# Two-layer graph kernel: beta added in the first layer, closing normalisation in two fused passes, last four tiles normalised where they are made, transposes issued ahead of the closing stores

## The reference, cut to what matters

```
h = relu(layernorm(x))
x = x + quantised_gnn(h, adj)                      # layer 0, gives x1
h = relu(layernorm(x))
for s in range(2):                                 # layer 1
    A  = softmax of the top-p entries of (Xa W1 W2)(Xa W3)^T
    Xf = R @ Xf ; Xa = A @ Xa
    Z  = Z + Xf @ U1s[s] + Xa @ U2s[s]
Y = h + Z
out = x1 + (Y - mean(Y)) * rsqrt(var(Y) + 1e-5) * gamma + beta
```

## Time and profile before

| | |
|---|---|
| median of 3 runs | 1310.68 us |
| lowest, highest | 1308.89, 1313.84 us |
| the profiled execution's own time | 1313.01 us |
| its span, first to last instruction | 1311.2 us |
| PE busy | 1116.9 us (85%) |
| DVE busy | 1036.7 us (79%) |
| ACT busy | 442.7 us (34%) |
| POOL busy | 260.5 us (20%) |
| chain that ended last | DVE 49%, PE 31%, issue 10%, ACT 4%, DMA 4% |

### The profile page before, as it was taken

One profiled execution on the slowest core, in us unless ns is written; L12 is line 12 of the kernel. 1 busy time (PEld: TensorE's weight loads), 2 busy tenths in 40 slices (PEclk: granted clock), 3 DMA queues, 4 the chain that ended last, 5 costly groups with the idle time before them and its releaser, 6 DMA issues.

```text
span 1311.2 us, 16604 instructions
## 1 busy us (share of the span) xinstructions
PE 1116.9 (85%) x5402; PEld 515.1 (39%) x5402; DVE 1036.7 (79%) x2199; ACT 442.7 (34%) x836; POOL 260.5 (20%) x234
## 2 busy tenths in 40 slices
PE   0567999999999798899997998989995997898374
PEld 0223555554334344344443443334442443343131
DVE  7887777762798998888884019979989998998777
ACT  2544545455533134444331255631420521100000
POOL 6023323231312112012121113122110121111011
PEclk9888999999999899899998999999997999899786
DMA  6126656552424531533524433176633733733576
GB/s 235 63 83 214 234 184 223 171 188 72 140 85 147 127 74 41 105 73 65 138 57 96 82 113 118 60 256 178 136 104 86 166 89 99 174 95 100 172 210 203
DMA packets 190931, 172.19 MB, mean 131 GB/s; under 512 B 144704, under 2 KB 144704, under 8 KB 186752
## 3 DMA queue, kind: packets, MB, share of 16 engines
q1 hardware_dynamic: 190848, 171.23, 45.6%
HBM read 88.10 MB, written 49.55 MB: 105 GB/s over the span
## 4 chain that ended last, share of the span: by engine, by line
DVE 49%; PE 31%; issue 10%; ACT 4%; DMA 4%; SPq 1%; POOL 1%; DVEq 1%; POOLq 0%; ACTq 0%
DVE cand L1679 7%; DVE WS L1461 6%; PE UB L745 5%; DVE WS L1676 5%; DVE E L1692 5%; DVE WS L1684 4%; PE AB L735 3%; PE AB L728 3%; DVE g L1541 3%; PE RB L745 3%; PE RB L912 3%; DVE E L1691 3%; PE XB L745 2%; PE AB L912 2%; DVE cand L1719 2%
## 5 line engine op out<-in xcount | busy, mean ns | idle before, releaser
L1541 DVE TENSOR_REDUCE g<-E 128x1 f32<-128x2048 f32 x32 | 73.0, 2281 | 96.9 <-ACT E L1135 96.7
L1461 DVE SCALAR_TENSOR_TENSOR WS<-E,g 128x2048 bf16<-128x2048 f32 x48 | 120.5, 2553 | 0.4
L632 POOL TENSOR_TENSOR RT<-RT,AD 128x512 f32<-128x512 f32 x32 | 57.4, 1792 | 293.2 <-ACT RT L1194 293.1
L1679 DVE MAX8 cand<-WS 128x8 f32<-128x128 f32 x512 | 102.1, 277 | 1.1
L1135 ACT ACTIVATE E<-LB 128x512 f32<-128x512 f32 x128 | 75.4, 593 | 75.7 <-PE LB L835 60.4
L912 PE MATMUL AB<-VR,turns 128*128 128x512 f16 x256 | 67.0, 409 | 33.2 <-DMA turns<-E 33.2
L912 PE MATMUL RB<-VR,turns 128*128 128x512 f16 x256 | 64.1, 395 | 30.7 <-DMA turns<-E 30.7
L1684 DVE SCALAR_TENSOR_TENSOR WS<-E,g 128x2048 f32<-128x2048 f32 x33 | 81.1, 2456 | 0.9
L1171 ACT ACTIVATE E<-E,nmx 128x2048 f32<-128x2048 f32 x32 | 63.7, 1993 | 46.7 <-DVE nmx L1542 46.6
L912 PE MATMUL RB<-XR,turns 128*128 128x512 f16 x256 | 63.8, 394 | 17.8 <-DMA turns<-E 17.8
L1692 DVE SCALAR_TENSOR_TENSOR E<-WS,E 128x2048 f16<-128x2048 f32 x32 | 77.9, 2433 | 1.1
(11 more groups left out here) (307 smaller groups left out, 2174.5 us busy)
## 6 DMA issues: line engine op xcount, KB each, us to landing
turns<-adj_parts SPq DMA_DIRECT2D x48, 512.0 KB, 3.8
E<-adjT SPq DMA_DIRECT2D x16, 1024.0 KB, 7.6
adj_parts<-turns SPq DMA_DIRECT2D x16, 1024.0 KB, 5.2
AH<-adj_parts SPq DMA_DIRECT2D x16, 512.0 KB, 4.1
z_d<-UO SPq DMA_DIRECT2D x31, 256.0 KB, 2.3
XR<-x SPq DMA_DIRECT2D x4, 1024.0 KB, 11.8
WS<-U SPq DMA_DIRECT2D x4, 1024.0 KB, 7.7
x_d<-E SPq DMA_DIRECT2D x16, 256.0 KB, 2.0
```

What stands on the lines that cost most here:

```text
L1461: return v.scalar_tensor_tensor(junk[t % 2], e, g4[:, k, t:t + 1], e, op, ALU.mult, accum_out=g4[:, F_, t:t + 1])
L1541: ct(v.tensor_reduce(row(A2)[:, t:t + 1], E[:, slot, :], AX.X, ALU.max))
L1679: i = v.max(cand[:, t, 8 * c:8 * c + 8], WS[:, c * PART:(c + 1) * PART])
```

## The change

**Beta.** beta is loaded at the start of the program (into `XHL`). In layer 0 a new POOL step `x1_beta` adds it to x1 of each tile (into `X1B`, which is `WF`), and SP stores that sum in place of x1. It stands in POOL's loop between the root and `x_lo`. DVE's next tile waits for this step instead of the store. The DVE additions of beta at the end are gone.

**Closing passes.** A tile's last four element-wise steps become two: `(y - mean) * gamma`, which doesn't need the root, and `y * root + (x1 + beta)`. Both are `scalar_tensor_tensor`, one instruction per tile.

**Last four tiles.** Tiles 12 to 15 aren't stored and loaded again. ACT and POOL write them to `UO` and `XF` in turn, and DVE normalises each there as a batch of one (`end`). Their x1 is loaded once into `WS` (`end_in`). DVE's order is batch 0, batch 1, tile 12, batch 2, tiles 13, 14, 15. ACT waits, for tiles 14 and 15, until the store of tile 12 or 13 has read the buffer.

**SP's order in the last group.** The first loads no longer wait for all tiles to be kept (`s_kept, 2 * T`), only for the transposes of the group before; `order` has memory of its own now, and gamma goes to `WF`. The store of batch 0 comes after the transposes of tile 13, and the loads of batch 2 and the store of batch 1 after those of tile 14.

**The register load.** DVE no longer waits for the group's first mask ahead of the register load; that wait now stands behind the skipped piece.

```
-        gb = sb("gb", [P, 2, D], F32)
-        gam, bet = gb[:, 0, :], gb[:, 1, :]
-        order = gb[:, :, :].rearrange("p a d -> p (a d)").bitcast(F16)
+        order = sb("order", [P, N], F16)[:, :]
+        bet, X1B = XHL[:, :, :].rearrange("p h d -> p (h d)").bitcast(F32), WF
+        gam, ends = WF, (UO, XF)
...
             u_in(0)
+            sp.dma_start(bet, beta.partition_broadcast(P)).then_inc(s_gb, 16)
...
             def l0_stores(t):
-                sp.wait_ge(s_x1, t + 1)
-                sp.dma_start(x1_d[t], X1T).then_inc(s_x1out, 16)
+                sp.wait_ge(s_x1b, t + 1)
+                sp.dma_start(x1_d[t], X1B[:, :]).then_inc(s_x1out, 16)
...
+            def end_in():
+                sp.wait_ge(s_kept, 2 * T)
+                sp.dma_start(end_x, x1_d[T - G:T].rearrange("t p d -> p t d")).then_inc(s_endx, 16)
+
+            def end_out(t, nth):
+                sp.wait_ge(s_res, nth)
+                sp.dma_start(out[t], ends[t % 2][:, :]).then_inc(s_end[t % 2], 16)
...
                 if last:
-                    sp.wait_ge(s_kept, 2 * T)
-                    sp.dma_start(bet, beta.partition_broadcast(P)).then_inc(s_gb, 16)
-                    sp.dma_start(gam, gamma.partition_broadcast(P)).then_inc(s_gb, 16)
+                    sp.wait_ge(s_wl, T)
+                    sp.wait_ge(s_gb, 16)
+                    sp.dma_start(gam[:, :], gamma.partition_broadcast(P)).then_inc(s_gb, 16)
...
-                    if s and t < T - 1:
+                    if s and not last:
                         y_store(t)
+                    if last and i == 0:
+                        end_in()
+                        fin_out(0, 1)
                     if last and i == 1:
-                        fin_out(0)
                         fin_in(2)
-                        fin_out(1)
+                        fin_out(1, 2)
                     if last and i == 2:
-                        fin_in(3)
-                        fin_in(4)
+                        end_out(T - G, 3)
+                        fin_out(2, 4)
+                    if last and i == 3:
+                        end_out(T - G + 1, 5)
...
+            def x1_beta(t):
+                pool.wait_ge(s_x1, t + 1)
+                pool.wait_ge(s_x1out, 16 * t + OPEN)
+                q.tensor_tensor(X1B[:, :], X1T, bet, ALU.add).then_inc(s_x1b, 1)
+
             def l0_tile(t):
                 l0(t)
+                x1_beta(t)
                 x_lo(t, of(XR, t))
...
-                    act.wait_ge(s_yout, 16 * t + OPEN)
-                    a(UO[:, :], bank[:, :], ACT.Copy, scale=rden[:, slot:slot + 1]).then_inc(s_ue, 1)
+                    act.wait_ge(s_yout, 16 * min(t, T - G) + OPEN)
+                    if t >= T - G + 2:
+                        act.wait_ge(s_end[t % 2], 16)
+                    y = ends[t % 2] if t >= T - G else UO
+                    a(y[:, :], bank[:, :], ACT.Copy, scale=rden[:, slot:slot + 1]).then_inc(s_ue, 1)
...
-                dve.wait_ge(s_x1out, 16 * t + OPEN)
+                dve.wait_ge(s_x1b, t)
...
-                ct(masked(tiles[0][0], 0, THR))
+                ct.free(masked(tiles[0][0], 0, THR))
+                first_kept = ct.base + ct.n
...
+                dve.wait_ge(c_dve, first_kept)
                 for slot, t in tiles:
...
+                for k, (m, y, x1) in enumerate(tiles):
+                    (ch if k == n - 1 else ch.free)(v.scalar_tensor_tensor(y, y, mv[:, m, 0:1], gam[:, :], ALU.subtract,
+                                                                           ALU.mult))
+                dve.wait_ge(s_frs, nth)
+                for k, (m, y, x1) in enumerate(tiles):
+                    i = v.scalar_tensor_tensor(y, y, frs[:, m:m + 1], x1, ALU.mult, ALU.add)
+                i.then_inc(s_res, 1)
...
+            batch(0, 1)
+            batch(1, 2)
+            dve.wait_ge(s_endx, 16)
+            end(T - G, 3)
+            batch(2, 4)
+            for k in range(1, G):
+                end(T - G + k, 4 + k)
```

More of the change, by code:

```diff
@@ L179, in build @@
         ZT = Khl[:, 0, 0:2 * D].bitcast(F32)
-        FIN = [(G * b, G * b + G) for b in range(NG - 1)] + [(T - G, T - 1), (T - 1, T)]
+        BATCHES = NG - 1
         fin_y = [E[:, 2 * h, :].rearrange("p (t d) -> p t d", t=G) for h in range(2)]
@@ L244, in build @@
             "s_zin", "s_y", "s_yout", "s_fvar", "s_frs", "s_res", "s_out")]
-        s_finx, s_finy = ([sem(f"{n}{h}") for h in range(2)] for n in ("s_finx", "s_finy"))
+        s_finx, s_finy, s_end = ([sem(f"{n}{h}") for h in range(2)] for n in ("s_finx", "s_finy", "s_end"))
+        s_endx = sem("s_endx")
         s_xin = [sem(f"s_xin{b}") for b in range(NG)]
@@ L665, in pairs @@
                         continue
+                    if g == NG - 1 and i == 0:
+                        root(0, 0, G)
+                    y = ends[t % 2] if g == NG - 1 else UO
                     pool.wait_ge(s_zin, 16 * t + 16)
                     pool.wait_ge(s_ue, t + 2 * T + 1 + OPEN)
-                    q.tensor_tensor(UO[:, :], UO[:, :], ZT, ALU.add).then_inc(s_y, 1)
+                    q.tensor_tensor(y[:, :], y[:, :], ZT, ALU.add).then_inc(s_y, 1)
                     if g == NG - 1:
-                        for b in ((i,) if i < G - 1 else (i, i + 1)):
-                            pool.wait_ge(s_fvar, b + 1)
-                            m = slice(*FIN[b])
-                            q.tensor_tensor(frs[:, m], frs[:, m], powc[:, 0, m], ALU.pow).then_inc(s_frs, 1)
+                        if i == 0:
+                            root(1, G, 2 * G)
+                        root(2 + i + (i > 0), t, t + 1)
+                        if i == 0:
+                            root(3, 2 * G, 3 * G)
             def last_post():
@@ new lines, in batch, with end @@
+            def batch(b, nth):
+                dve.wait_ge(s_finx[b % 2], 16 * (b // 2) + 16)
+                dve.wait_ge(s_finy[b % 2], 16 * (b // 2) + 16)
+                normed([(G * b + t, fin_y[b % 2][:, t, :], fin_x[b % 2][:, t, :]) for t in range(G)], nth)
+            def end(t, nth):
+                dve.wait_ge(s_y, t + 1 + OPEN)
+                normed([(t, ends[t % 2][:, :], end_x[:, t - (T - G), :])], nth)
+            dve.wait_ge(s_gb, 32)
+            batch(0, 1)
+            batch(1, 2)
```

79 lines of the change are left out of this document (33 added, 46 removed).

## The result

| | before | changed |
|---|---|---|
| median | 1311.91 us | 1299.53 us |
| lowest, highest | 1308.89, 1313.84 us | 1298.25, 1300.50 us |
| span of the profiled execution | 1311.2 us | 1296.3 us |

The ratio is 0.9907, 95% interval 0.9884 to 0.9930. The changed kernel is 12.4 us faster. The forecast was 1283.6 us with a range of 1277 to 1297, a gain of 27.1: the direction is right, the size is wrong, and the time lies outside the range.

What follows compares the result with a forecast made beforehand. It took PE as the bound in layer 0's tiles and layer 1's step 0 from 440 us, DVE in step 1. Gains 9.6 + 18.0 - 0.5 = 27.1 us, from 1310.7 to 1283.6 us; range 1277 to 1297.

Steps and rivals of the forecast that it cites:

- Part 1: Layer 1's groups: the register load runs while DVE is masking instead of behind it; gain 9.6 us, bounds 0 and 12.
- Rival (a): Register load: it waits for DVE to finish its mask, so its gain is nothing; time 1293 us, chance 0.15.
- The term for group 0 of step 0: Layer 1, register load: the overlap there counts through PE's wait at 440.86; gain 2.3 us.
- Parts 2 to 5: The end: earlier first loads, DVE's batches, second gap and work behind the last product; together 18.0 us gained, bounds 13 and 21.
- Rival (b): The end: tile 13's sum waits behind DVE's passes, batch 2 lands 4 us later; gain 11, time 1290 us, chance 0.07.
- Part 6: Layer 0: sixteen POOL sums for beta, 1.3 us each, cost 0.5 us, bounds 0 and 3.
- (c): Layer 0: the new sum gets the port only after DVE's long reduction; 11 us lost, time 1295 us, chance 0.04.
- (d): Layer 0: the sum waits for the reduction and another DVE instruction; 36 us lost, slower at 1320 us, chance 0.03.
- The sign that I named for part 6: Layer 0: a tile still takes 13.3 us, and `x_lo` ends before 213.5 in the tile shown.

## Why the prediction was wrong, point by point

**Part 1, the register load: mechanism right, 9.6 forecast, 4.8 to 5.8 measured.** The load starts 0.5 us behind the mask's start, as forecast, and the first halves of the last group 4.07 us behind it instead of the 3.2 forecast. Rival (a) is out. The term for group 0 of step 0 (2.3) was wrong: the wait at 440.86 is for the group's first tile, not tile 3, and hangs on SP's queue and not on DVE. The three groups of step 1 gave 5.9 and not 6.9, the last one 1.4 and not 2.3. The group with repairs gained 1.2 of its "issue" time (8.0 to 6.8), where I had 0.4.

**Parts 2 to 5, the end: right, 18.0 forecast, 17.0 measured alone** and 17.4 between the traces. Counted from tile 12's transposes, as the changed kernel is 2.4 late there: first load 6.6 (forecast 6.4), tile 13 24.5 (23.5), batch 0 done 27.7 (29.0), tile 15 58.9 (58.4), last store 77.3 (76.7). The tail from ACT's last copy is 5.2 (5.0). Rival (b) is out.

**Part 6, layer 0: 0.5 forecast, bounds 0 and 3, 10.0 measured. This is the step that failed**, and with it the prediction; with 10.0 in its place the sum would give 9.6 + 18.0 - 10.0 = 17.6, 1293.1, inside the range. Three things went wrong in it.

- I had the right row and didn't follow it. The earlier trace rows show a DVE instruction that took 1.03 us beside POOL's sum, and the text says that DVE might lose up to 1.3 us in each tile. DVE did lose 0.93 in each. Then the sum kept 0.5 "since PE is the bound in a tile and 3.5 us lie between `x_lo` and PE". That is the slack of POOL's `x_lo`, and the loss was DVE's. DVE's slack in a tile was 0.59 us, to be read from the starts of its normalisation, 12.75 us apart in the first tiles and 13.34 later.
- In the first tiles PE is not the bound at all, so there the whole 0.93 counts.
- Of the instructions behind the later store I named the adjacency load, which had room, and not the diagonal's store, behind which DVE waits. Loop 2 made 3.1 of the 9.8 us.

Rivals (c) and (d) were about this stretch, and (c)'s time, 1295, was nearest by luck. Both had POOL wait for DVE and PE for `x_lo`; in fact DVE waited for POOL, and ACT for DVE, and DVE again for the diagonal's store. The sum of (d) doesn't come out either: 209.5 + 7.3 + 1.2 puts `x_lo` at 218.0, 1.8 late and not 2.4, so 26 us and 1310. The sign that I named for part 6 shows the failure: a tile takes 13.97 us and not 13.3, while `x_lo` is in time.

## What to carry to other kernels

When work is put beside a running loop of several engines, price it on every engine that it can hold, each against that engine's own slack, and not against the slack of the engine that is the bound. A loop's hidden period can often be read where the bound isn't yet active: in the first turns. And between POOL and DVE the amount of work isn't all that counts, but also beside which DVE instruction it is put: the same 1.27 us cost 10 us beside the normalisation and 1.2 beside the statistics, where x1's store also goes 1.7 us earlier. Half the work beside the normalisation cost 1.5.
